# Delta-rule steps whose read takes the value as a seventeenth element, with one fold on GpSimd instead of two, and expert matmuls padded to 128 rows

## The reference, cut to what matters

```python
h = einsum('bsd,ehd->bseh', xn, w_up)          # 8 experts, top 2 per token, hidden size 704
val, gate = split(h, 2); h = val * silu(gate)
y = einsum('bseh,edh->bsed', h, w_down)

def step(S, inp):                              # 64 steps, state S is 16 x 16 for each image and head
    qt, kt, vt, at, bt = inp
    Sd = at[..., None, None] * S
    u = vt - einsum('bhk,bhkv->bhv', kt, Sd)
    Sn = Sd + bt[..., None, None] * kt[..., None] * u[:, :, None, :]
    o = einsum('bhk,bhkv->bhv', qt, Sn)
    return (Sn, o)
```

## Time and profile before

| what | value |
| --- | --- |
| median of 3 runs | 1418.88 us (1416.88 to 1424.58) |
| the profiled execution | 1413.77 us, of which the span from first to last instruction is 1412.1 us |
| mean granted TensorE clock | 0.915 of full |
| busy share of the span | PE 81%, PEld (weight loads) 60%, DVE 59%, ACT 40%, POOL 40% |
| expert tiles | about 262 to 580 us of the span |
| delta steps | 672 to 971 us, 64 steps |

### The profile page before, as it was taken

The page is one execution under the profiler, slowest core; times in us unless marked ns, Lnnn a source line. Parts: engine busy times, 40 slices in busy tenths (PEclk is TensorE's granted clock), DMA queues, the critical chain, the costliest instruction groups (busy, mean ns, idle before and its releaser), DMA issues. The chain is left out here.

```text
span 1412.1 us, 23993 instructions
## 1 busy us (share of the span) xinstructions
PE 1141.6 (81%) x8723; PEld 841.3 (60%) x8723; DVE 826.9 (59%) x1978; ACT 564.8 (40%) x1340; POOL 565.7 (40%) x626
## 2 busy tenths in 40 slices
PE   6999984898999999686667777774699999867854
PEld 4666662787889889532234444433577777645533
DVE  3666666211211211456999999997477777532886
ACT  2544552111111112155565666663234444325544
POOL 0111111232333233243699999995122222120657
PEclk9999995899999999799898999997799999979885
DMA  4111100988888887387000000001100040026601
GB/s 134 43 46 46 35 13 13 355 341 319 308 308 316 302 316 267 98 219 191 0 0 1 0 1 0 1 0 59 28 9 13 9 153 36 2 76 255 205 19 57
DMA packets 83349, 162.19 MB, mean 115 GB/s; under 512 B 44128, under 2 KB 62176, under 8 KB 77216
## 3 DMA queue, kind: packets, MB, share of 16 engines
q1 hardware_dynamic: 55536, 111.23, 23.0%
q0 software_dynamic: 10512, 45.10, 8.7%
q10 hardware_dynamic: 17184, 4.33, 1.4%
HBM read 134.28 MB, written 26.35 MB: 114 GB/s over the span
## 5 line engine op out<-in xcount | busy, mean ns | idle before, releaser
L1419 PE MATMUL banks<-made,ident 128*128 128x512 f32 x256 | 152.3, 680 | 91.2 <-DVE made L1630 90.6
L920 PE MATMUL banks<-rowsT,w_up 128*128 128x128 f32 x1716 | 201.3, 278 | 0.0
L920 PEld LDWEIGHTS banks<-rowsT,w_up 128*128 128x128 f32 x1716 | 198.0, 195 | 0.5 <-issue 0.3
L1682 POOL TENSOR_TENSOR ys<-xT_d,q_by_time 128x1024 f32<-128x1024 f32 x63 | 148.6, 2359 | 19.7 <-ACT xT_d L1502 9.8
L1525 ACT ACTIVATE banks<-banks,rate 128x256 f32<-128x256 f32 x256 | 103.9, 444 | 117.7 <-DVE made L1621 117.7
L1419 PEld LDWEIGHTS banks<-made,ident 128*128 128x128 f32 x256 | 41.5, 203 | 155.5 <-ACT banks L1525 130.3
L1686 POOL TENSOR_TENSOR ys<-ys 128x512 f32<-128x512 f32 x126 | 124.8, 990 | 9.9
L935 PE MATMUL banks<-w_down,hT 128*128 128x256 f32 x468 | 115.1, 388 | 0.6 <-DVE res L1100 0.6
L1090 DVE TENSOR_TENSOR hT<-banks,silu 64x128 f32<-64x128 f32 x39 | 11.0, 282 | 171.4 <-ACT silu L978 171.4
L864 POOL DMA_DIRECT2D w_down<-in_down_w x39 | 22.7, 583 | 199.8 <-PE banks L935 191.2
L935 PEld LDWEIGHTS banks<-w_down,hT 128*128 128x128 f32 x468 | 82.6, 189 | 22.0 <-issue 13.9
(11 more groups left out here) (312 smaller groups left out, 2305.8 us busy)
## 6 DMA issues: line engine op xcount, KB each, us to landing
w_up<-in_up_w SPq DMA_DIRECT2D x39, 1408.0 KB, 6.0
w_down<-in_down_w POOLq DMA_DIRECT2D x39, 768.0 KB, 5.6
inter<-res_x SPq DMA_DIRECT2D x16, 512.0 KB, 3.3
back<-inter SPq DMA_DIRECT2D x15, 512.0 KB, 3.9
patches<-in_patches SPq DMA_DIRECT2D x16, 384.0 KB, 3.3
f<-in_f SPq DMA_DIRECT2D x6, 1024.0 KB, 11.5
ys<-token_rows SPq DMA_DIRECT2D x16, 256.0 KB, 2.9
xn_rows<-xn_all SPq DMA_DIRECT2D x16, 128.0 KB, 1.7
```

Source lines behind the costliest of these rows:

```text
L920: ins = pe.matmul(out[:, m * P:(m + 1) * P], w[:, c, m * P:(m + 1) * P], x[:, c, :], start=(c == 0), stop=(c == 1))
L1419: pe.matmul(S[(t + 1) % 2][:, halves[h], :, :], ident[:, :], outer[:, halves[h], :, :], start=False, stop=True, skip_group_check=True).the ...
L1682: pool.tensor_tensor(qs[:, :, :, :], Sc[(t + 1) % 2][:, :, :, :], bcast(qt[:, t, :, :], 2, HD), ALU.mult).then_inc(sem("qs_made"), 1)
```

## The change

Experts: two memsets on GpSimd fill rows 64 to 127 of the sixth chunk of both `hT` buffers with zeros, ahead of its wait for the tile list; TensorE waits for them once, and the sixth chunk's product takes 128 rows like the others.

Delta steps: `prod` gets rows of 17 elements. VectorE's product fills the first 16; the scaled key has its sign turned; ScalarE copies the value into the seventeenth (`place_values`), so the sum over 17 is `u` and the subtraction goes. ScalarE's copy for step t + 1 stands between the fading and `copy_out` of step t, waits for `u_made{h}`, and it is now this copy that raises `faded{h}`. GpSimd folds once, 16 to 8. TensorE sums eight pieces instead of four, four after each half's `add_outer`; the four after h = 0 carry the waits for the fold and for `o_made`.

```diff
 
+        for p in range(2):
+            pool.memset(hT[p][HLAST:P, FULL, :], 0.0).then_inc(sem("h_padded"), 1)
         pool.wait_ge(sem("tile_at"), 1)
...
             for c in range(HIDC):
-                n = P if c < FULL else HLAST
-                ins = pe.matmul(Y, hT[j % 2][0:n, c, :], w_down[j % DEEP][0:n, c, :], start=(c == 0),
-                                stop=(c == FULL))
+                ins = pe.matmul(Y, hT[j % 2][:, c, :], w_down[j % DEEP][:, c, :], start=(c == 0), stop=(c == FULL))
             ins.then_inc(sem("y_made"), 1)
...
         up(0)
+        pe.wait_ge(sem("h_padded"), 2)
         for j in range(USED):
...
 LAST = TOK - CUTS[-1]
+FOLDED = HD // 2
 SUM_PARTS = ((0, 6), (6, 11), (11, HD))
...
     Sc = [by_state(xT[i][:, :, :].rearrange(states)) for i in range(2)]
-    prod, outer = (by_state(made_all[:, 2 * i:2 * i + 2, :].rearrange(states)) for i in range(2))
+    flat = made_all[:, :, :].rearrange(states)
+    n_prod, n_outer = CG * HD * (HD + 1), CG * HD * HD
+    prod = flat[:, 0:n_prod].rearrange("p (g v k) -> p g v k", g=CG, v=HD)
+    outer = by_state(flat[:, n_prod:n_prod + n_outer])
     squares = w[:, :, :].rearrange("p c n -> p (c n)")[:, 0:HD * CG * CUTS[1]].rearrange("p (d n) -> p d n", d=HD)
-    last_squares = made_all[:, 4:6, :].rearrange(states)[:, 0:CG * HD * LAST].rearrange("p (g d t) -> p g d t", g=CG, t=LAST)
+    last_squares = flat[:, n_prod + n_outer:n_prod + n_outer + CG * HD * LAST].rearrange("p (g d t) -> p g d t", g=CG, t=LAST)
     products = [by_state(front["ys"][:, 2 * i:2 * i + 2, :, :].rearrange("p n k d -> p (n k d)")) for i in range(2)]
...
     o_sum = banks[:, 5, 0:CG * HD].rearrange("p (g v) -> p g v", g=CG)
-    small = banks[:, 4, :].rearrange("p (n g v) -> p n g v", g=CG, v=HD)
-    read, u = small[:, 0, :, :], small[:, 1, :, :]
+    u = banks[:, 4, 0:CG * HD].rearrange("p (g v) -> p g v", g=CG)
     halves = [slice(2 * h, 2 * h + 2) for h in range(2)]
...
 
-        def add_outer(t):
-            for h in range(2):
-                pe.wait_ge(sem(f"faded{h}"), t + 1)
-                pe.wait_ge(sem(f"outer_made{h}"), t + 1)
-                pe.matmul(S[(t + 1) % 2][:, halves[h], :, :], ident[:, :], outer[:, halves[h], :, :], start=False,
-                          stop=True, skip_group_check=True).then_inc(sem(f"state{h}"), 1)
-
-        def sum_folded(t):
-            pe.wait_ge(sem("qs_folded"), 2 * t + 2)
-            if t:
-                pe.wait_ge(sem("o_made"), t)
-            for n in range(4):
-                ins = pe.matmul(o_sum, ident[:, :], products[t % 2][:, :, :, n], start=(n == 0), stop=(n == 3))
-            ins.then_inc(sem("o_folded"), 1)
+        def add_outer(t, h):
+            pe.wait_ge(sem(f"faded{h}"), t + 1)
+            pe.wait_ge(sem(f"outer_made{h}"), t + 1)
+            pe.matmul(S[(t + 1) % 2][:, halves[h], :, :], ident[:, :], outer[:, halves[h], :, :], start=False,
+                      stop=True, skip_group_check=True).then_inc(sem(f"state{h}"), 1)
+
+        def sum_folded(t, h):
+            if h == 0:
+                pe.wait_ge(sem("qs_folded"), t + 1)
+                if t:
+                    pe.wait_ge(sem("o_made"), t)
+            for n in range(FOLDED // 2 * h, FOLDED // 2 * (h + 1)):
+                ins = pe.matmul(o_sum, ident[:, :], products[t % 2][:, :, :, n], start=(n == 0),
+                                stop=(n == FOLDED - 1))
+            if h:
+                ins.then_inc(sem("o_folded"), 1)
 
...
         for t in range(TOK):
-            add_outer(t)
-            if t >= 2:
-                sum_folded(t - 2)
+            for h in range(2):
+                add_outer(t, h)
+                if t >= 2:
+                    sum_folded(t - 2, h)
             for n in range(CHUNKS_O):
...
                     sum_squares(n, t - CUTS[n + 1] - 6)
-        sum_folded(TOK - 2)
+        for h in range(2):
+            sum_folded(TOK - 2, h)
 
...
 
+        def place_values(t, h):
+            return act.copy(prod[:, halves[h], :, HD], v[:, halves[h], :, t])
+
         def copy_out(n, h):
...
         act.preload_act_table_set("natural_log_exp_and_others")
+        for g in range(CG):
+            act.wait_ge(sem(f"chain_v{g}"), 16)
+        for m in range(6):
+            act.wait_ge(sem(f"stored{m}"), 16 * CG)
+        for h in range(2):
+            place_values(0, h).then_inc(sem("values_placed"), 1)
         for t in range(TOK):
...
                                          scale=rate[:, g, 1, t:t + 1])
+                if t + 1 < TOK:
+                    act.wait_ge(sem(f"u_made{h}"), t + 1)
+                    ins = place_values(t + 1, h)
                 ins.then_inc(sem(f"faded{h}"), 1)
...
             once.settle()
-            once.mark(dve.tensor_tensor(f[:, 0, g % 2, :], rn[:, g, :], rate[:, g, 1, :], ALU.mult))
+            once.mark(dve.scalar_tensor_tensor(out=f[:, 0, g % 2, :], in0=rn[:, g, :], scalar=-1.0, in1=rate[:, g, 1, :],
+                                               op0=ALU.mult, op1=ALU.mult))
             once.settle()
...
         dve.wait_ge(sem("q_turned"), CG)
-        for g in range(CG):
-            dve.wait_ge(sem(f"chain_v{g}"), 16)
+        dve.wait_ge(sem("values_placed"), 2)
         for t in range(TOK):
-            now = slice(t, t + 1)
             for h in range(2):
...
                 dve.wait_ge(sem(f"state{h}"), t + 1)
-                dve.tensor_tensor(prod[:, at, :, :], S[t % 2][:, at, :, :], bcast(ka[:, t, at, :], 2, HD),
+                dve.tensor_tensor(prod[:, at, :, 0:HD], S[t % 2][:, at, :, :], bcast(ka[:, t, at, :], 2, HD),
                                   ALU.mult).then_inc(sem(f"prod_made{h}"), 1)
                 dve.wait_ge(sem(f"prod_made{h}"), t + 1)
-                dve.tensor_reduce(read[:, at, :], prod[:, at, :, :], AX.X, ALU.add
-                                  ).then_inc(sem(f"read_made{h}"), 1)
-                dve.wait_ge(sem(f"read_made{h}"), t + 1)
-                dve.tensor_tensor(u[:, at, :], v[:, at, :, now].rearrange("p g d o -> p g (d o)"),
-                                  read[:, at, :], ALU.subtract).then_inc(sem(f"u_made{h}"), 1)
+                dve.tensor_reduce(u[:, at, :], prod[:, at, :, :], AX.X, ALU.add).then_inc(sem(f"u_made{h}"), 1)
                 dve.wait_ge(sem(f"u_made{h}"), t + 1)
...
             dve.wait_ge(sem(f"state{h}"), TOK + 1)
-        once.mark(dve.tensor_tensor(prod[:, :, :, :], S[TOK % 2], bcast(qt[:, last, :, :], 2, HD), ALU.mult))
+        once.mark(dve.tensor_tensor(prod[:, :, :, 0:HD], S[TOK % 2], bcast(qt[:, last, :, :], 2, HD), ALU.mult))
         once.settle()
-        dve.tensor_reduce(o[:, :, :, last], prod[:, :, :, :], AX.X, ALU.add).then_inc(sem("last_o"), 1)
+        dve.tensor_reduce(o[:, :, :, last], prod[:, :, :, 0:HD], AX.X, ALU.add).then_inc(sem("last_o"), 1)
         mean_square(CHUNKS_O - 1)
...
             pool.wait_ge(sem("qs_made"), t + 1)
-            for i, n in enumerate((8, 4)):
-                pool.tensor_tensor(qs[:, :, :, 0:n], qs[:, :, :, 0:n], qs[:, :, :, n:2 * n],
-                                   ALU.add).then_inc(sem("qs_folded"), 1)
-                pool.wait_ge(sem("qs_folded"), 2 * t + i + 1)
+            pool.tensor_tensor(qs[:, :, :, 0:FOLDED], qs[:, :, :, 0:FOLDED], qs[:, :, :, FOLDED:2 * FOLDED],
+                               ALU.add).then_inc(sem("qs_folded"), 1)
 
```

## The result

The changed kernel takes 1399.45 us in the median of 5 runs (1397.68 to 1405.84), the kernel before 1418.88 (5 runs, 1414.55 to 1427.48): a ratio of 0.985, 95% interval 0.982 to 0.989. A second series of the changed kernel gave 1401.44 us beside 1418.18, 0.988 (0.985 to 0.992). Forecast were 1408.4 us, 1394 to 1425, and faster by over 0.5% with a chance of 0.58. The gain is 19.4 us in the first series and 16.7 in the second, where 10.5 were forecast.

The account below looks back on a forecast made before the run. It took TensorE to bound the expert tiles and a closed loop on VectorE the delta steps. Experts -10.5 us and steps 0 gave -0.74%, from the median 1418.9 to 1408.4 us, range 1394 to 1425.

Parts of the forecast that it names:

- The wait inside TensorE's queue: Delta steps: add_outer of h = 1 queues behind pieces waiting for ScalarE's store; step 4.58 us, sixty steps give 1.2 us.
- VectorE alone: Delta steps: without the subtraction a half takes 2.08 us, a step 4.17; 64 steps would give back 28 us.
- Experts: Expert tiles, sixth chunk: 128 rows instead of 64 remove the cost of changing rows; 10.5 us off.
- Squares: Nine delta steps: ten or twelve `sum_squares` matmuls ahead of add_outer of h = 0 delay its state; 3.5 us more.
- Clock: Delta steps: fewer stretches at TensorE's lower clock expected, -1 us; if all stay, they cost 6 us more.
- its own case: Whole kernel: steps at 4.47 to 4.80 us, experts 7.8 to 11 us; 1399 to 1422 us, chance 0.62.
- Slower by the price of the wait: Rival, delta steps: the wait costs more than priced, 4.90 us a step; about +9, 1428 us, chance 0.10.
- The full gain on VectorE: Rival, delta steps: the wait for `o_made` doesn't bind, VectorE's 2.08 us per half rule; 1384 us, chance 0.08.
- the padding gains nothing: Rival, expert tiles: longer intervals come from the chunk's place at a product's end, not its 64 rows; 1419 us, chance 0.07.
- The rival of the lower clock: Delta steps: every stretch at the lower clock stays and costs more; +7 on the sum, 1415.5 us, chance 0.13.

Follow-up runs that it names:

- two_sums: The changed kernel with two places for the summed output and all sums of squares in bank 6; 1379.61 us, ratio to the kernel before 0.971.
- split_6_2: The changed kernel with six pieces, not four, between the wait for `o_made` and the second half's add_outer, and two behind; 1434.11 us in one run.
- pad_only: The kernel before with only the expert padding, the delta steps as before; 1409.92 us beside 1418.18, ratio 0.994.
- sums_behind: The changed kernel with all eight pieces after both add_outers; 1378.26 us, ratio to the kernel before 0.971.

## Why the prediction was right, and where its size was off

- **The wait inside TensorE's queue** was right, and it is the finding: take the wait for the store away, in three ways, and the step falls from 4.56 to 4.17 us. Forecast 4.58 us a step, measured 4.56. By terms, of the step shown above: value copy to state copy 0.15 (0.14 forecast), store to first piece 862.78 to 862.92, 0.14 (0.08), the pieces 0.94 (0.96), add_outer and hand-over 1.09 (1.17). That the sum is right to 0.02 us is in part luck, as errors of +0.06 and -0.08 cancelled. VectorE alone would have 2.08 to 2.10 per half, as forecast, and has it in two_sums; there GpSimd's fold is what the pieces wait for next, also as forecast.
- **Experts**: 10.5 us forecast, 10.4 measured in the tiles, and the close match is in part luck. A tile gained 0.35 us, not the 0.285 at most of the forecast, because the turning of rows became shorter too (0.28 to 0.22); longer waits for gathered rows took some 3 us back, where the forecast allowed 0.6. The cause was named too narrowly. The Trainium skill's rule of "TensorEngine Tiling (Array Packing)", Key Properties, that a change of mode drains the engine, would cover the intervals at the two changes of rows, 0.31 and 0.30 us; it doesn't cover the 0.32 between two matmuls of 64 rows, which is longer as well. Padding removes them all, 0.29 us per product (2.88 to 2.59); what the engine does in them no run here shows.
- **Squares**: 3.5 forecast. In the changed kernel the three steps take 5.18, 4.62 and 4.89 instead of 4.56, about 1.0 per group, 3.0 in all.
- **Clock** is the term that was mis-sized, and most of what makes the forecast 9 us too high. I took -1 us, from one profile whose two waits showed 2.0 us, and put +6 beside it as the other end. At 4.60 us a step the old loop would last 63 x 4.60 + 2.30 = 292.1 us; the five profiles of it have 298.0 in the mean, so the stretches at the lower clock cost 5.9 us there, 3.2 even in the profile that I read. The new steps have next to none behind the first 13 us of the loop. That makes 298.0 - 291.2 = 6.8 us for the delta steps instead of 0, and with the padding's 10.4 it is 17.2 of the 19.4 measured. The measured 1399.45 us lies at the very edge of the 1399 to 1422 that the prediction gave its own case. One argument for the -1 was also miscounted: with eight pieces instead of four TensorE has 16 small matmuls a step instead of 8, not 32 instead of 16.
- **How well the parts are known.** By the medians of one series of runs the padding alone gives 8.3 us (interval 4.5 to 11.5), the delta steps alone 4.6 (2.0 to 9.2), both together 16.7. So each part is known to some 3 us only, and the runs put the delta steps below the profiles' 6.8; that they gain at all, where 0 was forecast, both show.
- **Rivals.** Slower by the price of the wait: the shape was right (split_6_2 is slower than before, at 5.01 us a step), the price was not reached. The full gain on VectorE did not come; one wait hides 20 us of it. That the padding gains nothing is refuted by pad_only. The rival of the lower clock went the other way.

The stretch after the loop, with the same code in all kernels, took 441.8 us in sums_behind and 451.6 in pad_only. Their busy time there, with the granted clock third from the end:

```profile
932.90:1374.70 441.80, 344.67 (x3429) 263.04 (x3427) 276.36 (x759) 177.25 (x428) 128.43 (x218) 0.87 0.22 74
```

```profile
958.70:1410.30 451.60, 352.16 (x3406) 268.07 (x3405) 276.44 (x760) 177.24 (x428) 129.81 (x219) 0.84 0.21 72
```

TensorE is busy 7.5 us longer for the same matmuls at the lower clock, so up to 10 us between two profiles need not come from a change.

What stays open: whether it is the additional matmuls or the closed gap that keeps the clock up in the new loop (split_6_2 speaks for the gaps, but changes the length of the step too); what lengthens the intervals around the matmuls of 64 rows; and why the stretch after the loop gets a lower clock in one execution than in another.

## What to carry to other kernels

When small work is moved between two links of a recurrence on an in-order engine, its waits move too: ask for each which engine releases it, and where in the same step that happens. Here a store at the end of ScalarE's step took back 20 of the 27 us that the new steps win without it (298.0 to 270.7), and moving either side by one place returned them. One profile is not enough to price a state that comes and goes, like the granted clock: read several of the kernel before, and the granted clock of all its runs. Rows of the same kind of instruction elsewhere in the trace price a new chain well, here each term to within 0.08 us and their sum to 0.02 in 4.56.

## What the runs showed that I had not expected

TensorE's clock fell in the old loop to the lower level at places that differ between executions of the same program, though its idle time ahead of an add_outer is only some 1.2 us, and the loop's time differed by 7 us for it; with 16 more small matmuls per step it was 1.00 in all three profiles. And a pair of matmuls of 64 rows is slow by itself (0.32 us apart, where 128 rows take 0.22), not only at its borders.
